# Gates of a selective scan: three of four channel groups go from VectorE to ScalarE and GpSimd

## The chip, the core and the metric

One core of a Trainium2 chip runs the whole program. The metric is the device time of one execution in microseconds (us), the median of several executions. Engines are named as in the profile: PE (TensorE; PEld are its weight loads), DVE (VectorE), ACT (ScalarE), POOL (GpSimd) and SP (which only issues transfers).

## The reference

The input x is 2 sequences of 2048 rows of 256 numbers. After a layer norm, two branches are computed, and their sum is added to x. One branch is a mixture of 16 experts, two chosen for each row. The other is a selective scan over 512 channels with 16 states each:

```
xz = x @ W_in;  x_in, z = split(xz)
u = silu(causal_conv4(x_in) + conv_b)
delta = softplus(dt_lr @ W_dt + b_dt)          # dt_lr, B, C = split(u @ W_xproj)
h_t = exp(delta_t * A) * h_{t-1} + delta_t * u_t * B_t
y_t = sum_n h_t[:, n] * C_t[n]  +  D_skip * u_t
out = (y * silu(z)) @ W_out
```

The change touches the last product, `y * silu(z)`, called the gate here.

## The kernel before

**Chunks and units.** The 4096 rows are cut into 8 chunks (0 to 7) of 512 rows. A chunk has 4 channel groups (`dc` = 0 to 3) of 128 channels, which lie on the partitions, and each group has 16 states. One state of one group of one chunk is a unit, a tile of 128 x 512: 64 units for each chunk, 512 in all. A unit goes through four engines:

- ACT computes the decay exp(delta * A) into `hb`, a ring of 12 units (L846). In program order it is 6 units ahead.
- DVE multiplies du by B into `psB` (L1632) and runs the scan in place in `hb` (L1643), unit after unit.
- POOL multiplies two units at a time by C into `hc`, a ring of 6 units (L658, called a pair here). Ten of the 256 pairs are DVE's (L1652).
- PE adds each unit of `hc` to the sum of its group with four transposing matmuls (L1150, `sum_unit`), four units later in its program. Groups take turns in two PSUM banks, `psY[dc % 2]`. Before its first unit a group's bank is started with D_skip * u (L1163, `dskip`).

ACT can write unit g of `hb` only when POOL has read unit g - 12, and POOL can write unit g of `hc` only when PE has summed unit g - 6.

**Slots.** Everything else is woven in by hand. Each engine's program is a loop over chunks and slots 0 to 63 (one for each unit), and the tables `AT`, `AT0` (chunk 0) and `AT7` (chunk 7) say after which slot an engine does which step; a name that `AT0` or `AT7` lacks is taken from `AT`. A slot is a place in the order of each engine's program, not a time: an engine gets there when all before it is done, and each engine executes strictly in order. The steps that matter here:

- **The projections of the next chunk.** They share one bank, `psA`, so PE and ACT alternate on it: x_in, convolution and silu (L1169, L1177 on PE, L780, L792, L799 on ACT), z (L1225 on PE, L869 and L874 on ACT, the last with silu at slot 28), and at slots 50 to 61 and 3 of the next chunk the four delta projections (`d_mm`, L1213 on PE), each followed by ACT's relu, exp and ln in the scratch tile `tmpA` (L828, L830, L835) and DVE's `d_max` (L1457), which reads `psA` and `tmpA`. `d_mm` of one group waits for `d_max` of the group before.
- **The gate** (L1659 on DVE): `zs[:, :, group] *= psY[dc % 2]`. It waits for silu(z) and for the last sum of its group. Groups 0 to 2 stand at slots 30, 45, 54 (`AT`), 34, 41, 52 (`AT0`) and 37, 41, 53 (`AT7`), and group 3 at slot 3 of the next chunk (slot 2 of chunk 7). It also frees its bank for the next but one group's `dskip`.
- **The output of a chunk.** `y_tr` on PE (L1233) transposes the gated tile once all its groups are gated, `y_copy` on ACT (L885), `o_mm` on PE (L1240), `o_copy` on ACT (L893) into `om`, four times, and then one accumulating transfer issued by POOL (L712) adds `om` to the output. For chunks 0 to 6 this is done in slots 4 to 17 of the next chunk. For chunk 7, three groups are done inside the chunk from slot 48 on, the last after the loop (L1429, L1438, L1695).
- **The experts.** 20 groups of 4 tiles, from unit 93 on: PE L1249, L1264, L1267, L1276, L1286, L1290, ACT L899, L906, L956, L967 (gelu, with a table load ahead and behind), L980. POOL adds each tile to the output with an indirect transfer (L707); each such transfer waits until the one before has landed, and an accumulating transfer of a chunk counts in the same row. In chunks 0 and 1 POOL also scatters 64 + 16 row tiles (L673, L681).

POOL also multiplies delta by u (L666, 128 x 512, both operands in SBUF), four times in each chunk.

## Time and profile before

| | |
|---|---|
| time, median of 3 executions | 1123.73 us (1122.23 to 1125.07) |
| profiled execution, first to last instruction (its span) | 1114.4 us |
| median less span: launch and end, outside of the trace | 9.3 us |
| busy share of the span | DVE 93%, PE 84%, POOL 79%, ACT 78% |
| mean granted clock of PE | 0.925 of full |

No time of its own is on record for the profiled execution beyond its span; the 9.3 us are taken as constant. All times in the trace are us from the first instruction. A row of a timeline is start, duration, engine, line, operation and count of a merged run of instructions; in brackets stands how long the engine sat idle before it, and what released it. The loop over chunks begins at about 62 us and ends at about 1105 us; chunk 5, which is read closely below, runs on DVE from about 723 to 848 us.

### The profile page before, as it was taken

To read this page: it belongs to the slowest core of one execution; us is meant where nothing else is said; L and a number is where in the kernel's file an instruction comes from. 1 tells how busy PE (TensorE), PEld (TensorE's weight loads), DVE (VectorE), ACT (ScalarE), POOL (GpSimd) and SP (SyncE) were. 2 spreads that over 40 slices of the span, in tenths; PEclk is the share of its full clock that TensorE was granted. 3 is DMA by queue.
4 is the path that set the end of the run, shared out by engine and by line. 5 is a ranking of instruction groups with operands and counts; after the bars stand their busy time and mean duration, and the time that the engine had idled before them with its cause. 6 is when DMAs were issued, how large, how long until landed. Compare 5 with 4: busy or idle time off the path is not lost.

```text
span 1114.4 us, 16950 instructions
## 1 busy us (share of the span) xinstructions
PE 930.9 (84%) x4575; PEld 630.4 (57%) x4575; DVE 1036.3 (93%) x1304; ACT 867.0 (78%) x1841; POOL 881.2 (79%) x570
## 2 busy tenths in 40 slices
PE   5947766587979999789998999899989999787776
PEld 3424434454656656566666766576656665565564
DVE  7999999799999988997899979999999999899995
ACT  4574788465897799767999699978998798976981
POOL 7178999599777887858787878887897886877995
PEclk9968986698999999899999999799998999899988
DMA  9496568953484544824457553763367443764313
GB/s 328 175 342 227 161 194 290 331 183 92 117 283 153 114 102 143 307 49 95 119 166 278 104 139 75 274 190 72 81 191 266 100 105 92 243 213 114 77 20 66
DMA packets 119367, 185.86 MB, mean 167 GB/s; under 512 B 12012, under 2 KB 104344, under 8 KB 111016
## 3 DMA queue, kind: packets, MB, share of 16 engines
q1 hardware_dynamic: 87120, 144.60, 38.8%
q0 software_dynamic: 19584, 25.26, 13.1%
q10 hardware_dynamic: 12568, 14.93, 4.4%
q8 instruction: 36, 0.59, 0.2%
q14 instruction: 59, 0.48, 0.1%
HBM read 146.34 MB, written 42.60 MB: 170 GB/s over the span
## 4 chain that ended last, share of the span: by engine, by line
PE 36%; issue 16%; ACT 15%; DVE 13%; POOL 11%; DMA 5%; ACTq 2%; SPq 1%; POOLq 0%; DVEq 0%
DVE hb L1643 10%; POOL hc L658 7%; PE psY L1150 7%; PE psA L1177 5%; PE psC L1290 4%; ACT hb L846 4%; PE psC L1240 3%; PE psA L1225 3%; PE psA L1169 2%; PE psE L1267 2%; ACT hnT L967 2%; DVE psB L1632 2%; POOL out L707 2%; DMA Cb<-bc_d 2%; DMA xs_d<-xg,slots 2%
## 5 line engine op out<-in xcount | busy, mean ns | idle before, releaser
L658 POOL TENSOR_TENSOR hc<-hb,Cb 128x1024 f32<-128x1024 f32 x246 | 623.8, 2630 | 83.3 <-PE psY L1150 64.4
L1643 DVE TENSOR_TENSOR_SCAN hb<-hb,carry,psB 128x512 f32<-128x512 f32 x384 | 471.8, 1263 | 7.7 <-ACT hb L846 6.1
L1150 PE MATMUL psY<-ident,hc 128*128 128x128 f32 x2048 | 306.9, 291 | 76.3 <-POOL hc L658 76.2
L846 ACT ACTIVATE hb<-delta,aneg 128x512 f32<-128x512 f32 x512 | 351.5, 716 | 21.7 <-POOL hc L658 15.7
L1150 PEld LDWEIGHTS psY<-ident,hc 128*128 128x128 f32 x2048 | 255.1, 150 | 191.0 <-POOL hc L658 109.4
L1632 DVE TENSOR_TENSOR psB<-Bb,psU 128x512 f32<-128x512 f32 x510 | 323.7, 679 | 0.5 <-DMA Bb<-bc_d 0.5
L707 POOL DMA_INDIRECT out<-yo,idx x80 | 128.0, 1600 | 55.3 <-DMA out<-yo,idx 18.0
L1643 DVE TENSOR_TENSOR_SCAN hb<-hb,psB 128x512 f32<-128x512 f32 x128 | 149.2, 1200 | 2.1 <-ACT hb L846 2.1
L1177 PE MATMUL psA<-ux,dgw 128*128 128x512 f32 x232 | 113.7, 610 | 3.0 <-ACT ux L786 2.0
L1290 PE MATMUL psC<-w2r,hnT 128*128 128x256 f32 x320 | 90.0, 430 | 0.0
L1267 PE MATMUL psE<-w1r,xgT 128*128 128x256 f32 x320 | 82.9, 404 | 0.0
L1290 PEld LDWEIGHTS psC<-w2r,hnT 128*128 128x128 f32 x320 | 63.9, 210 | 18.5 <-issue 10.0
L1267 PEld LDWEIGHTS psE<-w1r,xgT 128*128 128x128 f32 x320 | 59.3, 195 | 16.2 <-issue 9.3
L1169 PE MATMUL psA<-xnT,win 128*128 128x512 f32 x116 | 59.0, 626 | 11.2 <-ACT zs L876 5.0
L967 ACT ACTIVATE hnT<-hnT,vecs 128x128 f32<-128x128 f32 x160 | 64.2, 481 | 1.2 <-issue 0.7
L1225 PE MATMUL psA<-win,xnT 128*128 128x512 f32 x128 | 61.2, 600 | 3.0 <-ACT zs L869 2.2
L1240 PE MATMUL psC<-wout,ygT 128*128 128x256 f32 x248 | 59.8, 383 | 1.2 <-ACT ygT L885 0.8
L1177 PEld LDWEIGHTS psA<-ux,dgw 128*128 128x128 f32 x232 | 41.4, 198 | 31.9 <-issue 26.3
L673 POOL DMA_INDIRECT xs_d<-xg,slots x37 | 40.9, 1104 | 19.2 <-DMA xg<-xn_d 11.4
L1213 PE MATMUL psA<-xr,rows 16*128 16x512 f32 x60 | 40.7, 763 | 15.0 <-DVE delta L1457 14.3
L980 ACT ACTIVATE yo<-psC,wv 128x256 f32<-128x256 f32 x80 | 33.3, 468 | 21.2 <-PE psC L1290 21.2
L666 POOL TENSOR_TENSOR du<-delta,ux 128x512 f32<-128x512 f32 x31 | 44.6, 1438 | 6.6 <-DVE delta L1457 4.4
(235 smaller groups left out, 1205.8 us busy)
## 6 DMA issues: line engine op xcount, KB each, us to landing
Bb<-bc_d SPq DMA_DIRECT2D x32, 1024.0 KB, 6.7
Cb<-bc_d SPq DMA_DIRECT2D x32, 1024.0 KB, 7.5
w1r<-w1c_d SPq DMA_DIRECT2D x80, 256.0 KB, 2.8
w2r<-in_L_ffn_W SPq DMA_DIRECT2D x80, 256.0 KB, 3.5
xg<-xs_d SPq DMA_DIRECT2D x20, 516.0 KB, 5.8
xg<-xn_d SPq DMA_DIRECT2D x37, 128.0 KB, 2.9
Bb<-in_L_attn_x SPq DMA_DIRECT2D x8, 512.0 KB, 7.5
xn_d<-hb SPq DMA_DIRECT2D x8, 512.0 KB, 8.9
```

The costliest lines, as they stand in the source:

```text
L658: pool.tensor_tensor(hc[:, k:k + 2, :], hb[:, g % HR:g % HR + 2, :], Cb[:, n:n + 2, :], ALU.mult).then_inc(s_g, 1)
L707: pool.indirect_dma_start(out=out[:, :], out_offset=bass.IndirectOffsetOnAxis(ap=idx[:, g % 2, j:j + 1], axis=0), in_=yo[:, j, :], in_offs ...
L846: act.activation(hb[:, g % HR, :], delta[:, dc, :], ACT.Exp, scale=aneg[:, dc, n:n + 1]).then_inc(s_exp, 1)
L967: ins = act.activation(hnT[:, j, kc, :], hnT[:, j, kc, :], ACT.Gelu, scale=g1t[:, bass.ds(e, 1), kc], bias=be1t[:, bass.ds(e, 1), kc])
L1150: mm = pe.matmul(y[:, tt * P:(tt + 1) * P], hc[:, g % GR, tt * P:(tt + 1) * P], ident[:, :], start=False, stop=(n == NS - 1), is_transpose ...
L1177: mm = pe.matmul(bank[:, :], dgw[:, dc, k, :], x_of(p, dc)[:, k:k + T], start=(k == 0), stop=(k == KW - 1))
L1225: mm = pe.matmul(psA[:, :], xnT[:, c % 2, kc, tt * P:(tt + 1) * P], win[:, 1, kc, :], start=(kc == 0), stop=(kc == KC - 1))
L1240: mm = pe.matmul(psC[:, 0:D], ygT[:, dc, :], wout[:, dc, :], start=(dc == 0), stop=(dc == dc_out(c) - 1))
L1267: mm = pe.matmul(psE[:, a * D:(a + 1) * D], xgT[:, a, kc, :], w1r[:, a, kc, :], start=False, stop=(kc == KC - 1), skip_group_check=True)
L1290: mm = pe.matmul(psC[:, a * D:(a + 1) * D], hnT[:, 2 * h + a, kc, :], w2r[:, 2 * h + a, kc, :], start=False, stop=(kc == KC - 1), skip_gro ...
L1632: dve.tensor_tensor(psB[g % 2][:, :], Bb[:, n, :], psU[:, :], ALU.mult).then_inc(s_dbu, 1)
L1643: dve.tensor_tensor_scan(h, h, psB[g % 2][:, :], first, ALU.mult, ALU.add).then_inc(s_scan, 1)
```

## The change

DVE keeps the gate of group 3. For groups 0 to 2, ACT copies the sum out of its bank into SBUF (`y_evict`, slots 21, 37 and 53 of every chunk), and POOL multiplies `zs` by the copy, in place (`gate`, slots 30, 42 and 57; in chunks 0 and 7 the slots of before stay). No new buffer is made: the copy of groups 0 and 1 goes to `tmpA`, that of group 2 to the first half of `om`. So ACT's copy of group 1 waits for POOL's gate of group 0, and the relu of the next chunk's delta waits for POOL's gate. `dskip` now waits for ACT's copy instead of DVE's gate, and `y_tr` waits for POOL's gates.

```
-    "gate": [30, 45, 54, 3],
+    "gate": [30, 42, 57, 3],
...
+    "yev": [21, 37, 53],
...
+        def y_free(j):
+
+            c, dc = divmod(j, DC)
+            return (s_gate, c + 1) if dc == DC - 1 else (s_yev, c * (DC - 1) + dc + 1)
+
+        def yraw(dc):
+
+            return om[:, 0:2, :].rearrange("p a d -> p (a d)") if dc == 2 else tmpA[:, :]
...
+            def gate(c, dc):
+                pool.wait_ge(s_z, c + 1)
+                pool.wait_ge(s_zc, (c + 1) * TT)
+                pool.wait_ge(s_yev, c * (DC - 1) + dc + 1)
+                z = zs[:, :, dc * P:(dc + 1) * P]
+                pool.tensor_tensor(z, z, yraw(dc).rearrange("p (a b) -> p a b", a=TT), ALU.mult).then_inc(s_gp, 1)
...
+                        for dc in at(c, "gate", s, 0, DC - 1):
+                            gate(c, dc)
...
+                if p > 0 and dc < 2:
+                    act.wait_ge(s_gp, (p - 1) * (DC - 1) + dc + 1)
                 act.activation(tmp, bank_d(p, dc)[:, :], ACT.Relu, bias=col(bneg, dc), scale=-1.0).then_inc(s_de, 1)
...
+            def y_evict(c, dc):
+
+                act.wait_ge(s_tr, c * UN + (dc + 1) * NS)
+                if dc == 0:
+                    act.wait_ge(s_delta, (c + 1) * DC)
+                elif dc == 1:
+                    act.wait_ge(s_gp, c * (DC - 1) + 1)
+                elif c > 0:
+                    act.wait_ge(s_acc, 16 * ADD_TURN["chunk", c - 1, 0])
+                act.activation(yraw(dc), psY[dc % 2][:, :], ACT.Copy).then_inc(s_yev, 1)
...
             def dskip(c, dc):
                 j = c * DC + dc
                 if j >= 2:
-                    pe.wait_ge(s_gate, j - 1)
+                    pe.wait_ge(*y_free(j - 2))
...
             def y_tr(c, tt):
                 bank_c("y", c, tt)
-                pe.wait_ge(s_gate, c * DC + dc_out(c))
+                pe.wait_ge(s_gp, (c + 1) * (DC - 1))
+                if dc_out(c) == DC:
+                    pe.wait_ge(s_gate, c + 1)
...
-            def gate(c, dc):
+            def gate(c):
+                dc = DC - 1
                 dve.wait_ge(s_z, c + 1)
                 dve.wait_ge(s_zc, (c + 1) * TT)
-                dve.wait_ge(s_tr, c * UN + (dc + 1) * NS)
+                dve.wait_ge(s_tr, (c + 1) * UN)
```

**ACT in chunk 5, around slot 37.** The rows are ACT's order there, first before, then changed (lines of the changed file are larger; L800 and L1000 are the L780 and L967 of before).

```order
L780 ACTIVATE ux<-psA 128x512
L786 ACTIVATE ux<-psA 128x3
L963 TENSOR_LOAD etab
L963 ISA x2
L967 ISA
L967 REGISTER_ALU
L967 ACT_TABLE_LOAD
L967 ACTIVATE hnT<-hnT,vecs 128x128
```

```order
L800 ACTIVATE ux<-psA 128x512
L806 ACTIVATE ux<-psA 128x3
L885 ACTIVATE tmpA<-psY 128x512
L996 TENSOR_LOAD etab
L996 ISA x2
L1000 ISA
L1000 REGISTER_ALU
L1000 ACT_TABLE_LOAD
L1000 ACTIVATE hnT<-hnT,vecs 128x128
```

The copy of group 1 now stands between ACT's part of the convolution input and the gelu of an expert group with its table load.

**POOL in chunk 7, from slot 36 to the end.** Before, then changed; L658 and L669 are the pairs, L707 and L725 the experts' adds, L712 and L730 the add of the chunk, L684 the gate.

```order
L658 TENSOR_TENSOR hc<-hb,Cb 128x1024 x2
L707 DMA out<-yo,idx 4225x256
L658 TENSOR_TENSOR hc<-hb,Cb 128x1024 x3
L707 DMA out<-yo,idx 4225x256
L658 TENSOR_TENSOR hc<-hb,Cb 128x1024
L707 DMA out<-yo,idx 4225x256
L658 TENSOR_TENSOR hc<-hb,Cb 128x1024 x2
L707 DMA out<-yo,idx 4225x256
L658 TENSOR_TENSOR hc<-hb,Cb 128x1024 x2
L707 DMA out<-yo,idx 4225x256
L658 TENSOR_TENSOR hc<-hb,Cb 128x1024
L712 DMA out<-om 128x4x256
```

```order
L684 TENSOR_TENSOR zs<-zs,tmpA 128x4x128
L669 TENSOR_TENSOR hc<-hb,Cb 128x1024
L725 DMA out<-yo,idx 4225x256
L669 TENSOR_TENSOR hc<-hb,Cb 128x1024 x3
L725 DMA out<-yo,idx 4225x256
L669 TENSOR_TENSOR hc<-hb,Cb 128x1024
L725 DMA out<-yo,idx 4225x256
L669 TENSOR_TENSOR hc<-hb,Cb 128x1024
L684 TENSOR_TENSOR zs<-zs,om 128x4x128
L669 TENSOR_TENSOR hc<-hb,Cb 128x1024
L725 DMA out<-yo,idx 4225x256
L669 TENSOR_TENSOR hc<-hb,Cb 128x1024 x2
```

The pair between the last two experts' adds of the first piece (`x2`) is parted by the gate of group 2 in the second: it now stands between pair 52 and pair 54. The gates of groups 0 and 1 stand a little earlier.

**PE in chunk 7, at slot 51.** Before, then changed, with the semaphores that each waits for (`s_g`: POOL's pairs, `s_gate`: DVE's gates, `s_gp`: POOL's gates).

```order
L1150 MATMUL psY<-ident,hc 128x128 [waits s_g]
L1150 MATMUL psY<-ident,hc 128x128 x3
L1233 MATMUL psC<-ident,zs 128x128 [waits s_gate,s_c]
L1233 MATMUL psC<-ident,zs 128x128 x2
L1150 MATMUL psY<-ident,hc 128x128 [waits s_g]
L1150 MATMUL psY<-ident,hc 128x128 x3
```

```order
L1185 MATMUL psY<-ident,hc 128x128 [waits s_g]
L1185 MATMUL psY<-ident,hc 128x128 x3
L1270 MATMUL psC<-ident,zs 128x128 [waits s_gp,s_c]
L1270 MATMUL psC<-ident,zs 128x128 x2
L1185 MATMUL psY<-ident,hc 128x128 [waits s_g]
L1185 MATMUL psY<-ident,hc 128x128 x3
```

The order on PE is the same; the first `y_tr` of chunk 7, which stands between the sums of units 47 and 48, waits for POOL's third gate instead of DVE's.

## Rows read from the trace of the kernel before

**Rows 1.** The page: busy time of each engine, share of the span, instructions

```profile
PE 930.9 (84%) x4575; PEld 630.4 (57%) x4575; DVE 1036.3 (93%) x1304; ACT 867.0 (78%) x1841; POOL 881.2 (79%) x570
```

**Rows 2.** Groups by line: shapes xcount | busy us, mean ns | idle before <-releasers

```profile
L658 POOL TENSOR_TENSOR hc<-hb,Cb 128x1024 f32<-128x1024 f32 x246 | 623.8, 2630 | 83.3 <-PE psY L1150 64.4 <-DVE hb L1643 17.6
L1643 DVE TENSOR_TENSOR_SCAN hb<-hb,carry,psB 128x512 f32<-128x512 f32 x384 | 471.8, 1263 | 7.7 <-ACT hb L846 6.1 <-ACT carry L858 1.5
L1632 DVE TENSOR_TENSOR psB<-Bb,psU 128x512 f32<-128x512 f32 x510 | 323.7, 679 | 0.5 <-DMA Bb<-bc_d 0.5
...
L1659 DVE TENSOR_TENSOR zs<-zs,psY 128x512 f32<-128x512 f32 x32 | 21.4, 669 | 29.1 <-ACT zs L874 17.0 <-PE psY L1150 10.1 <-ACT zs L876 2.0
...
L869 ACT ACTIVATE zs<-psA 128x512 f32<-128x512 f32 x24 | 14.3, 595 | 10.0 <-PE psA L1225 10.0
```

**Rows 3.** POOL's line L666: duration ns min/median/max, first and last start

```profile
L666 POOL TENSOR_TENSOR du<-delta,ux x31: 1085/1284/1926, 92.0 to 1045.0; 128x512 f32<-128x512 f32 x31
```

**Rows 4.** Busy by window: PE, PEld, DVE, ACT, POOL, clock, DMA share, GB/s

```profile
269.00:299.00 30.00, 26.27 (x121) 15.77 (x120) 30.00 (x36) 21.46 (x42) 24.07 (x16) 0.94 0.42 125
781.00:813.00 32.00, 29.83 (x139) 19.21 (x138) 30.32 (x37) 31.18 (x61) 26.35 (x18) 1.00 0.34 80
813.00:844.00 31.00, 25.86 (x120) 16.41 (x119) 31.00 (x37) 28.23 (x57) 28.80 (x15) 0.79 0.78 248
```

**Rows 5.** Timeline, chunk 5 at slots 30 to 40: DVE, ACT, PE, POOL

```profile
784.51 0.69 DVE L1659 TENSOR_TENSOR zs<-zs,psY 128x512 f32<-128x512 f32 x1 [1.68 <-ACT zs L874]
...
796.44 1.28 ACT L967 ACT_TABLE_LOAD   x1
...
802.23 0.60 ACT L899 ACTIVATE xgT<-psC 128x512 f32<-128x512 f32 x1
...
802.89 0.39 PE L1286 MATMUL psC<-rows,pick 6*128 6x512 bf16 x1 [1.29 <-ACT xgT L899]
...
808.02 2.36 POOL L658 TENSOR_TENSOR hc<-hb,Cb 128x1024 f32<-128x1024 f32 x1 [5.02 <-PE psY L1150]
```

**Rows 6.** Timeline, chunk 5 at slots 54 to 60: POOL, then PE

```profile
832.25 7.52 POOL L658 TENSOR_TENSOR hc<-hb,Cb 128x1024 f32<-128x1024 f32 x3
841.47 2.36 POOL L658 TENSOR_TENSOR hc<-hb,Cb 128x1024 f32<-128x1024 f32 x1 [1.71 <-DVE hb L1643]
...
835.22 1.11 PE L1150 MATMUL psY<-ident,hc 128*128 128x128 f32 x4 [1.56 <-POOL hc L658]
837.89 2.07 PE L1213 MATMUL psA<-xr,rows 16*128 16x512 f32 x2 [1.56 <-DVE delta L1457]
```

**Rows 7.** Timeline, end of chunk 0: POOL, ACT, DVE

```profile
187.17 1.81 POOL L673 DMA_INDIRECT xs_d<-xg,slots  x1 [0.17 <-issue]
...
204.42 0.20 ACT L923 ACTIVATE xg<-meta 128x2 f32<-128x2 f32 x1 [10.93 <-DMA xs_d<-xg,slots]
...
207.26 0.75 DVE L1457 SCALAR_TENSOR_TENSOR delta<-psA,vecs,tmpA 128x512 f32<-128x512 f32 x1 [7.64 <-ACT tmpA L835]
```

**Rows 8.** Timeline of POOL, from the end of chunk 6 to the end

```profile
980.49 1.58 POOL L707 DMA_INDIRECT out<-yo,idx  x1 [3.26 <-DMA out<-yo,idx]
...
1028.90 1.68 POOL L707 DMA_INDIRECT out<-yo,idx  x1 [5.22 <-DMA out<-om]
...
1059.89 2.37 POOL L658 TENSOR_TENSOR hc<-hb,Cb 128x1024 f32<-128x1024 f32 x1 [0.83 <-PE psY L1150]
...
1085.97 2.35 POOL L658 TENSOR_TENSOR hc<-hb,Cb 128x1024 f32<-128x1024 f32 x1 [0.25 <-PE psY L1150]
...
1093.05 2.35 POOL L658 TENSOR_TENSOR hc<-hb,Cb 128x1024 f32<-128x1024 f32 x1 [0.60 <-DVE hb L1643]
...
1099.69 1.39 POOL L712 DMA_DIRECT2D out<-om  x1
```

**Rows 9.** Timeline of PE, chunk 7 at its first y_tr

```profile
1082.48 0.52 PE L1233 MATMUL psC<-ident,zs 128*128 128x128 f32 x3 [4.36 <-DVE zs L1659]
```

More of the change, by code:

```diff
@@ L386, in build @@
         s_c = sem("s_c")
+        s_yev, s_gp = sem("s_yev"), sem("s_gp")
         s_xT, s_xi, s_xq, s_xp, s_xe, s_u, s_xd, s_xr, s_bco = (sem(n) for n in (
@@ L1106, in _ @@
                         z_silu(c)
+                    for dc in at(c, "yev", s):
+                        y_evict(c, dc)
                     if c > 0:
@@ L1424, in _ @@
                 sum_unit(g)
-            pe.wait_ge(s_gate, NC * DC)
+            pe.wait_ge(s_gate, NC)
             pe.wait_ge(s_c, len(C_TURN))
@@ L1683, in _ @@
                                 d_max(c, 3)
-                        for dc in at(c, "gate", s, 0, DC - 1):
-                            gate(c, dc)
                         if c > 0:
                             for _ in at(c, "gate", s, DC - 1, DC):
-                                gate(c - 1, DC - 1)
-            gate(NC - 1, DC - 1)
+                                gate(c - 1)
+            gate(NC - 1)
             dve.wait_ge(s_fa, 16)
```

## The prediction

> **What bounds the kernel now.** I read the page first. DVE is busy for 93% of the span, the other three for 78 to 84% [rows 1]. That asks for DVE to be relieved, but busy shares average over stages, so the second view was the groups by line. DVE's own two operations of a unit take 1263 and 679 ns, a pair of units nearly 3.9 us by these means, and POOL's pair 2630 ns [rows 2]. POOL has its other work (du products, indirect transfers) beside this, so it is not far behind. The same view says what DVE waits for at its gates: 17.0 us for silu(z), 10.1 us for PE's last sums, and 2.0 us for the last quarter of silu(z) [rows 2].
>
> The third view, busy time by window, shows two regimes. In chunk 1 DVE is busy for all of its 30.00 us while POOL has 6 us free (the first of [rows 4]). From chunk 2 on the experts run as well. In chunk 5 at slots 32 to 48 ACT is busy for 31.18 of 32.00 us, and at slots 48 to 63 POOL is busy for 28.80 of 31.00 (the second and third of [rows 4]). There the engines pass the lead around, and the timeline shows how. PE's work on the projections ends in silu(z), for which DVE's gate of group 0 waits 1.68 us [rows 5]. ACT then does a gelu between two table loads and one copy more; PE waits for that copy until 802.89, and POOL waits 5.02 us for PE until 808.02 [rows 5]. From there POOL works through until it waits for DVE at 841.47 [rows 6]. PE waits for POOL at 835.22 and right afterwards for DVE's `d_max` until 837.89, by 1.56 us [rows 6]. With that `d_mm` the next round of projections starts. So DVE is the last of the chain in chunk 5 by only 1.56 us.
>
> **What is removed.** 24 DVE gates of 669 ns, 16.1 us in all, and with them the waits for silu(z), 17.0 + 2.0 = 19.0 us [rows 2]; the 10.1 us stay, as I put them with group 3, whose gate stays. If DVE were the bound all along, this would give 35.1 us.
>
> **What is added.** On ACT, 24 copies of a 128 x 512 bank to SBUF. The like of it, L869, takes 595 ns [rows 2], so 14.3 us. On POOL, 24 products of 128 x 512 from two SBUF tiles. L666 is the same operation and shape: 1085 at least, 1284 in the middle, 1926 at most [rows 3]. The long ones overlap what follows, so I take 1.2 us, 28.8 us in all, with 1.1 and 1.9 as ends. No transfer is added.
>
> The GPSIMD Engine Reference of the Trainium skill, in its section on elementwise work, speaks against such a move: VectorE is roughly 2x faster, and a two-input operation costs about 2.6 cycles for each element there. That would be an estimate of 1.1 us for 512 elements at 1.2 GHz before dispatch, 26.6 us for 24. The trace agrees: 1284 against 669 ns is 1.9 times.
>
> **What of it lies on the path, chunk by chunk.**
>
> *Chunk 0.* POOL is in arrears with its scatter when chunk 0 ends: the scatter issued at 187.17 has landed when ACT goes on at 204.42, and DVE waits 7.64 us at `d_max` for what ACT was held from [rows 7]. Three gates push that scatter back by up to 3 x 1.2 = 3.6 us. The transfers around it are what it waits for, so its landing need not move as much. Bounds 0 and +3.6; I take the third of it, **+1.2**. DVE's own 2.0 us less there are lost in its wait.
>
> *Chunk 1.* DVE has no wait, POOL has room [rows 4]. 3 x 0.67 = **-2.0**. Nothing is given back before chunk 2's projections start, since they start from DVE's `d_max`.
>
> *Chunks 2 to 5.* By chunk 5. The gate of group 0 on POOL is covered: it ends before POOL's wait of 5.02 us [rows 5]. ACT's copy of group 1 stands directly before the table load at 796.44; all behind it is ACT's own work up to the copy for which PE waits 1.29 us [rows 5]. So 0.6 us pass on to PE and, at 808.02, to POOL. The gate of group 1 comes after 808.02 where POOL no longer waits: 1.2 us. Together +1.8 for pair 54, which ended at 832.25 + 7.52 / 3 = 834.8 [rows 6]. DVE by now is 1.68 + 3 x 0.67 = 3.7 us early, but PE must first sum unit 54. Its start moves from 837.89 only by 1.8 - 1.56 = **+0.2**, and DVE's earliness turns into a wait of `d_max` or of a scan. The gate of group 2 comes after pair 56 and falls into POOL's wait of 1.71 us at 841.47, so it costs nothing; without that wait it would cost 1.2. Four chunks: **+0.8**. The longest of the five waits for silu(z) has more to give than the others (17.0 us by five are 3.4 each, that of chunk 5 is 1.68). DVE can use of it only what decays ACT has in stock, so I take **-1.0** for all four chunks together, with -8 as the far end.
>
> *Chunk 6.* ACT's 0.6 us as before. The gate of group 2 falls into a row of transfers that wait for one another: POOL waits 3.26 us at 980.49 for the last one to land [rows 8], so it passes on, 1.2. **+1.8**.
>
> *Chunk 7.* POOL is released at 1028.90 by the add of chunk 6, and from there to the end its only waits over 0.2 us are 0.83, 0.25 and 0.60 us [rows 8]. DVE hardly holds it up. The gates of groups 0 and 1: 2.4 - 0.83 = +1.6. The third gate is the costliest. PE's first `y_tr` waited 4.36 us for DVE's gate until 1082.48 [rows 9], when POOL was at pair 52. Now this gate comes after pair 52. Behind the waiting `y_tr` on PE stand the sums from unit 48 on, and pair 54 may be written only after unit 49 is summed. So between pairs 52 and 54 come 1.2 us for the gate, then on PE 0.5 for the three matmuls of `y_tr` [rows 9] and, at that rate, some 1.0 for the eight of two sums: 2.7 where there was 0.25 [rows 8]. That is +2.4, less the 0.60 of waiting for DVE that goes away: +3.4 in all for POOL. The four rounds of `y_tr`, copy, `o_mm`, copy start some 6 us later than at 1082.48 (pair 52 ended 0.25 us before 1085.97, at 1085.7 [rows 8]; + 1.6 + 1.2 = 1088.5). They took until POOL could issue the add of the chunk at 1099.69 [rows 8], with little to spare, so the add comes later than POOL alone would have it, and all that ends the kernel with it. Bounds +3.4 and +6; I take **+4.5**.
>
> Sum: 1.2 - 2.0 + 0.8 - 1.0 + 1.8 + 4.5 = +5.3. The span of 1114.4 becomes 1119.7; with the 9.3 us around it that is 1129.0 us. The median of before is 1123.73 = 1114.4 + 9.3, so it is the same sum.
>
> **The rivals.**
>
> *DVE is what counts (faster).* For it speaks the 93% and that DVE is the last in line at 837.89 [rows 1, 6]. If POOL hides its gates, because its waits for PE shrink by as much as it is late, chunks 2 to 6 each gain 2.0 for the gates and 1.7 for the wait, less ACT's 0.6: 3.1 x 5 = 15.5. With -2.0 of chunk 1, +1.2 of chunk 0 and, since POOL keeps up, +1.6 in chunk 7, this gives 1123.7 - 14.7 = 1109.0. It decides where POOL can end pair 54 earlier by more than the 1.2 of a gate. Against it: POOL was busy from 808.02 on [rows 6], and 28.80 of 31.00 us [rows 4]. The full 35.1 us would be 1088.6, which I exclude, since ACT is already full at slots 32 to 48.
>
> *No change.* The shares in the middle chunks cancel, the longest wait for silu(z) gives 3 instead of 1, and the end costs its lower bound: about 1124.
>
> *ACT is what counts (slower by more).* ACT waits in order at each copy for PE's sum. If its three copies and their waits all lie on the way of the projections, six chunks pay 3 x 0.6 instead of 0.6, +7.2 more, and the gates take 1.9 us instead of 1.2 at the five places where they are not covered, +3.5 more: 1140. Against it: at slots 21 and 53 ACT has waits for PE to hide a copy in.
>
> **How the numbers follow.** Forecast (+1 to +11, 1125 to 1135) 0.48, faster 0.28, no change 0.16, slower by more 0.08. About 0.3% (3.4 us) is what a measurement can tell from no change. A small part of the forecast's case (up to +3.4) is within it, 0.06, and the no-change case gives 0.13 to same and 0.03 to faster. Faster 0.31, same 0.19, slower 0.50. The range reaches down to the faster rival (1109) and up to nearly the slower one: 1110 to 1137. The likeliest case's own range is 1125 to 1135.
>
> **What the profile after would show.** DVE busy some 16 us less, no more waits at gates 0 to 2, but longer waits at `d_max` (for ACT's ln) and for decays. POOL's gates near 1.2 us, ACT's copies near 0.6. POOL further behind DVE at slots 44 to 56. In chunk 7, PE waiting for POOL's gate at the first `y_tr` some 6 us later than before, then pair 54 waiting for PE, and the chunk's add issued about 5 us later. Wrong would be: chunks 2 to 6 shorter by 3 us each, POOL waiting for DVE rather than DVE for the others, or a chunk 0 that ends at a quite different time because its scatters landed otherwise.

## The result and the profile after

| | median | executions |
|---|---|---|
| before | 1122.98 us | 4 (1121.57 to 1125.07) |
| after | 1132.58 us | 4 (1131.94 to 1135.39) |
| ratio after / before | 1.0107, 95% interval [1.0074, 1.0141] | |

The changed kernel is slower by 1.07%, about 12 us. The ratio is not that of the two medians in the table, which lie 9.6 us apart (0.85%); its interval holds both. Here and below a per cent is that of the ratio on record, and us are worked out from it at 1120 us. The forecast said slower (1129.0, +5.3 us), its range held the time, and the size was half of what came.

Two things about the spans first. The profiled execution of after took 1135.39 us with a span of 1133.4: only 2.0 us lie around the span, not 9.3. So the profiled execution of before, with its span of 1114.4, took about 1116.4, some 7 us less than its median. Spans of the two profiles therefore differ by 19.0 us where the kernels differ by about 12. PE's mean granted clock was 0.925 in that execution of before, where 98 others of that kernel on three chips had 0.907 to 0.922, and 0.916 in that of after. Ratios below come from many executions; profiles are used for what happens within a stretch.

Busy time of each engine, from the page of after, which answers to [rows 1]:

```profile
PE 938.5 (83%) x4574; PEld 636.4 (56%) x4575; DVE 1030.4 (91%) x1280; ACT 877.4 (77%) x1865; POOL 909.1 (80%) x594
```

POOL has 27.9 us more and ACT 10.4 more. DVE has lost 24 gates of 669 ns and yet only 5.9 us. What it waits for is in its groups by line, the answer to [rows 2] (scan, `d_max`, gate of group 3, after busy and mean the idle time ahead):

```profile
L1680 DVE TENSOR_TENSOR_SCAN hb<-hb,carry,psB 128x512 f32<-128x512 f32 x384 | 473.2, 1269 | 28.9 <-ACT hb L868 21.4 <-ACT carry L891 7.5
L1680 DVE TENSOR_TENSOR_SCAN hb<-hb,psB 128x512 f32<-128x512 f32 x128 | 149.7, 1206 | 6.8 <-ACT hb L868 6.8
L1494 DVE SCALAR_TENSOR_TENSOR delta<-psA,vecs,tmpA 128x512 f32<-128x512 f32 x30 | 22.1, 738 | 23.7 <-ACT tmpA L857 23.7
L1697 DVE TENSOR_TENSOR zs<-zs,psY 128x512 f32<-128x512 f32 x8 | 5.4, 681 | 19.5 <-PE psY L1185 19.5
```

The same groups of the kernel before that [rows 2] lack (the scans of chunk 0, `d_max`, DVE's own pairs):

```profile
L1643 DVE TENSOR_TENSOR_SCAN hb<-hb,psB 128x512 f32<-128x512 f32 x128 | 149.2, 1200 | 2.1 <-ACT hb L846 2.1
L1457 DVE SCALAR_TENSOR_TENSOR delta<-psA,vecs,tmpA 128x512 f32<-128x512 f32 x30 | 22.0, 733 | 16.9 <-ACT tmpA L835 16.9
L1652 DVE TENSOR_TENSOR hc<-hb,Cb 128x1024 f32<-128x1024 f32 x10 | 16.9, 1691 | 3.8 <-PE psY L1150 3.5
```

The waits for silu(z) are gone. Scans waited 7.7 + 2.1 us, mostly for ACT's decays, and now 28.9 + 6.8; `d_max` 16.9 and now 23.7. DVE is early and stands waiting a little further on.

The durations of the added work, from the lines of POOL's gate and ACT's copy for groups 0 and 1 (min/median/max in ns):

```profile
L684 POOL TENSOR_TENSOR zs<-zs,tmpA x16: 1254/1740/1865, 145.7 to 1079.7; 128x512 f32<-128x512 f32 x16
...
L885 ACT ACTIVATE tmpA<-psY x16: 573/600/615, 113.5 to 1072.5; 128x512 f32<-128x512 f32 x16
```

The copy is the 0.6 us of the forecast. POOL's record of a gate often reads 1.8 us, but the gate at 1079.65 below is followed by a pair at 1080.89: 1.24 us. Wherever a pair follows a gate at once it starts 1.22 to 1.24 us after it. Before a transfer POOL takes longer (824.27 to 826.25 below), and it will matter that whoever waits for the gate's result waits for the end of the record.

Busy time by window, answering to the second and third of [rows 4]; the windows are moved by 4 and 8 us, about as chunk 5 is:

```profile
785.00:817.00 32.00, 30.23 (x137) 19.36 (x136) 31.97 (x37) 30.94 (x55) 26.78 (x18) 0.95 0.37 92
821.00:852.00 31.00, 24.69 (x120) 14.76 (x119) 28.49 (x34) 28.00 (x58) 30.50 (x17) 0.87 0.69 213
```

In the second of these, POOL is busy for 30.50 us of 31.00 (28.80 before) and DVE for 28.49 (31.00 before). The timeline of chunk 5, POOL, PE, ACT and DVE, answers to [rows 5, 6]:

```profile
824.27 1.82 POOL L684 TENSOR_TENSOR zs<-zs,tmpA 128x512 f32<-128x512 f32 x1
826.25 1.59 POOL L725 DMA_INDIRECT out<-yo,idx  x1 [0.17 <-issue]
...
830.28 0.66 PE L1185 MATMUL psY<-ident,hc 128*128 128x128 f32 x4 [1.25 <-POOL hc L669]
...
833.22 0.38 ACT L939 ACTIVATE xgT<-psE 128x256 f32<-128x256 f32 x1 [1.45 <-PE psE L1304]
...
818.99 1.28 DVE L1680 TENSOR_TENSOR_SCAN hb<-hb,carry,psB 128x512 f32<-128x512 f32 x1 [2.02 <-ACT carry L891]
838.70 0.75 DVE L1494 SCALAR_TENSOR_TENSOR delta<-psA,vecs,tmpA 128x512 f32<-128x512 f32 x1 [2.51 <-ACT tmpA L857]
```

DVE had no wait at 818.99 before; its only one around there was the 1.68 us for silu(z) at slot 30 [rows 5]. Before, PE waited at slot 54 for DVE's `d_max` [rows 6]; now `d_max` waits for ACT (838.70), which had waited for PE (833.22), which had waited for POOL (830.28). The gate of group 1 at 824.27 lies in POOL's full stretch.

Timeline of chunk 7, POOL, PE and DVE, answering to [rows 8, 9]:

```profile
1079.65 1.83 POOL L684 TENSOR_TENSOR zs<-zs,tmpA 128x512 f32<-128x512 f32 x1
1080.89 2.90 POOL L669 TENSOR_TENSOR hc<-hb,Cb 128x1024 f32<-128x1024 f32 x1
...
1097.85 2.92 POOL L669 TENSOR_TENSOR hc<-hb,Cb 128x1024 f32<-128x1024 f32 x1
1100.15 1.84 POOL L684 TENSOR_TENSOR zs<-zs,om 128x512 f32<-128x512 f32 x1
1104.86 2.35 POOL L669 TENSOR_TENSOR hc<-hb,Cb 128x1024 f32<-128x1024 f32 x1 [2.87 <-PE psY L1185]
...
1102.13 0.87 PE L1270 MATMUL psC<-ident,zs 128*128 128x128 f32 x3 [8.25 <-POOL zs L684]
1102.79 4.24 PE L1185 MATMUL psY<-ident,hc 128*128 128x128 f32 x20
...
1123.92 0.69 DVE L1697 TENSOR_TENSOR zs<-zs,psY 128x512 f32<-128x512 f32 x1 [13.62 <-PE psY L1185]
```

This is what the forecast drew: PE's first `y_tr` waits for POOL's gate (8.25 us instead of 4.36), and the pair behind the gate then waits 2.87 us for PE. DVE, done early, waits 13.62 us for the last sum.

Two rows of before belong beside this, POOL's pair 52 and a window at PE's first matmuls after its wait (PE's granted clock is the last number but two):

```profile
1082.77 2.95 POOL L658 TENSOR_TENSOR hc<-hb,Cb 128x1024 f32<-128x1024 f32 x1
...
1082.40:1083.30 0.90, 0.82 (x8) 0.85 (x9) 0.90 (x2) 0.26 (x1) 0.90 (x2) 1.00 0.00 0
```

The same window after:

```profile
1102.10:1104.80 2.70, 2.67 (x13) 2.70 (x14) 2.70 (x4) 1.10 (x2) 0.00 (x0) 0.50 0.02 6
```

Before, `y_tr` ran at full clock (2.4 GHz); after, having waited 8.25 us, PE did `y_tr` and the sums that pair 54 needs at the lower of its two levels (1.2 GHz).

### The profile page after: what moved, and what is told of

The parts are those of the page before. It is cut to its first block and busy times, and to the rows that moved or that the text cites. A ratio compares the mean times of both kernels' runs of the same rounds, so it can differ in the third digit from the quotient of the medians.

```text
span 1133.4 us, 16997 instructions
## 1 busy us (share of the span) xinstructions
PE 938.5 (83%) x4574; PEld 636.4 (56%) x4575; DVE 1030.4 (91%) x1280; ACT 877.4 (77%) x1865; POOL 909.1 (80%) x594
## 5 line engine op out<-in xcount | busy, mean ns | idle before, releaser
L669 POOL TENSOR_TENSOR hc<-hb,Cb 128x1024 f32<-128x1024 f32 x246 | 629.6, 2648 | 85.0 <-PE psY L1185 62.4
L1680 DVE TENSOR_TENSOR_SCAN hb<-hb,carry,psB 128x512 f32<-128x512 f32 x384 | 473.2, 1269 | 28.9 <-ACT hb L868 21.4
L725 POOL DMA_INDIRECT out<-yo,idx x80 | 128.0, 1599 | 50.7 <-issue 16.8
L1000 ACT ACTIVATE hnT<-hnT,vecs 128x128 f32<-128x128 f32 x160 | 64.2, 481 | 1.0 <-issue 0.6
L926 ACT ACTIVATE om<-psC 128x256 f32<-128x256 f32 x32 | 12.2, 382 | 49.0 <-PE psC L1277 46.6
L1277 PEld LDWEIGHTS psC<-wout,ygT 128*128 128x128 f32 x248 | 45.9, 195 | 7.4 <-ACT ygT L918 2.1
```

Of the source, the lines that this page charges most:

```text
L669: pool.tensor_tensor(hc[:, k:k + 2, :], hb[:, g % HR:g % HR + 2, :], Cb[:, n:n + 2, :], ALU.mult).then_inc(s_g, 1)
L725: pool.indirect_dma_start(out=out[:, :], out_offset=bass.IndirectOffsetOnAxis(ap=idx[:, g % 2, j:j + 1], axis=0), in_=yo[:, j, :], in_offs ...
L1000: ins = act.activation(hnT[:, j, kc, :], hnT[:, j, kc, :], ACT.Gelu, scale=g1t[:, bass.ds(e, 1), kc], bias=be1t[:, bass.ds(e, 1), kc])
L1277: mm = pe.matmul(psC[:, 0:D], ygT[:, dc, :], wout[:, dc, :], start=(dc == 0), stop=(dc == dc_out(c) - 1))
L1680: dve.tensor_tensor_scan(h, h, psB[g % 2][:, :], first, ALU.mult, ALU.add).then_inc(s_scan, 1)
```

## The experiments

All kernels are made from one that has both kinds of gate and a list that says which are moved. A gate that is not moved stands on DVE at its slot of before, and who waits for it is switched with it. With an empty list every engine's order of instructions is that of before, with the full list that of after. Each ratio is to the kernel before on the same chip, with its 95% interval. There are twelve, on three chips: chunk 7 only, all but chunk 7, gates left out and products alone on the first; copies alone, group 2 of chunk 7, group 1 kept and group 0 alone on the second; the other four on the third.

```
+MOVED = [(c, dc) for c in range(NC) for dc in range(DC - 1) if moved(c, dc)]
...
+            return (s_yev, MOVED_N[c, dc]) if (c, dc) in MOVED_N else (s_gate, KEPT_N[c, dc])
```

### Which chunks: only chunk 7, and all but chunk 7

```
+moved = lambda c, dc: c == NC - 1
```

> Only chunk 7's three gates are moved to ACT and POOL; chunks 0 to 6 are as before. My theory (the end is the costliest place: POOL has no slack left there and PE's first y_tr now waits for a gate behind pair 52) says most of the loss is here. The prediction priced it at +4.5 us; the trace after the change, where POOL's shift against before grows by some 8 us between slot 32 of chunk 7 and the end, says +8, so 1127 to 1131. Rival (the loss builds up evenly, chunk by chunk, from the copies and the products): an eighth of the 9.6 us, about 1124.

Measured: 1.0056 [1.0027, 1.0085].

```
+moved = lambda c, dc: c < NC - 1
```

> The complement: chunks 0 to 6 moved, chunk 7's gates stay on VectorE. My theory: 1132.6 less 5 to 8 = 1125 to 1128, what stays being the losses of chunks 0, 3 and 6. Rival (even): 1131. A third view (VectorE relief works and only the end spoils it): at or below 1120.

Measured: 1.0058 [1.0037, 1.0078]. The two add up to 1.14%, the whole change has 1.07%. So about half of the loss is in chunk 7 (6.3 us, with 3.0 to 9.5 in its interval) and half in the seven chunks ahead of it (6.5 us, 4.1 to 8.7). For these seven my own sum had 0.8 us.

### What the relief alone is worth: gates of groups 0 to 2 left out

This kernel leaves `y * silu(z)` out for groups 0 to 2; nothing takes its place, PE's `y_tr` waits for silu(z) instead, and `dskip` of a bank that such a group leaves waits for no gate.

```
             def gate(c, dc):
-                if (c, dc) not in KEPT_N:
+                if dc < DC - 1:
                     return
```

> The relief of VectorE by itself: the 24 gates of groups 0 to 2 are left out altogether (the product with silu(z) is missing there), with nothing added on ACT or POOL; PE's y_tr waits for silu(z) directly. My theory (VectorE is last in line by only 1 to 2 us in each chunk, except in chunk 1 and at the end): -6 to -14 us, 1109 to 1117. Rival (VectorE is the bound all along): the full 35 us, 1088 to 1093. If this came out near 1123, even free gates would bring nothing.

Measured: 0.9984 [0.9962, 1.0007]. This is the run that surprised me most. 16.1 us of work and 19.0 us of waits are taken from the engine that is busy for 93% of the span, and 1.8 us come back, which can't be told from none (the interval reaches from 4.3 us won to 0.8 lost). Its groups by line, of DVE, say where they went:

```profile
L1694 DVE TENSOR_TENSOR_SCAN hb<-hb,carry,psB 128x512 f32<-128x512 f32 x384 | 471.8, 1263 | 27.3 <-ACT hb L878 20.5 <-ACT carry L901 6.6
L1694 DVE TENSOR_TENSOR_SCAN hb<-hb,psB 128x512 f32<-128x512 f32 x128 | 149.4, 1202 | 5.8 <-ACT hb L878 5.8
L1508 DVE SCALAR_TENSOR_TENSOR delta<-psA,vecs,tmpA 128x512 f32<-128x512 f32 x30 | 22.0, 734 | 24.8 <-ACT tmpA L867 22.4 <-issue 2.4
...
L1712 DVE TENSOR_TENSOR zs<-zs,psY 128x512 f32<-128x512 f32 x8 | 5.4, 676 | 14.6 <-PE psY L1196 14.6
```

Scans wait 33.1 us where it was 9.8, `d_max` 24.8 where it was 16.9, the gate of group 3 14.6 where PE's sums had 10.1: 35.7 us of new waits for 35.1 freed (in a span that is 5.6 us longer, so some of it is of this execution). These are the waits of after, although nothing was added to ACT and POOL. In chunk 2 the exchange can be read row by row. DVE before:

```profile
394.27 0.69 DVE L1659 TENSOR_TENSOR zs<-zs,psY 128x512 f32<-128x512 f32 x1 [2.40 <-ACT zs L874]
...
403.94 2.45 DVE L1643 TENSOR_TENSOR_SCAN hb<-hb,carry,psB 128x512 f32<-128x512 f32 x2 [0.71 <-ACT hb L846]
```

and without the gate:

```profile
404.43 2.45 DVE L1694 TENSOR_TENSOR_SCAN hb<-hb,carry,psB 128x512 f32<-128x512 f32 x2 [3.82 <-ACT hb L878]
```

2.40 of waiting, 0.69 of gate and 0.71 of waiting become one wait of 3.82 us at a scan 10 us later, and that scan starts at 404.43 instead of 403.94.

### What the added work alone costs: products alone, copies alone

DVE keeps all its gates. In the first kernel POOL does 24 products of 128 x 512 at the gates' slots, from a constant into `tmpA` or `om`, which are overwritten later; those who write there wait for it. In the second ACT makes the 24 copies; nothing reads them, but DVE's gate of the group waits for the copy, so this is a little more than ACT's time.

```
+                            w = dgw[:, 0, :, :].rearrange("p a b -> p (a b)")
+                            pool.tensor_tensor(yraw(dc), w, w, ALU.mult).then_inc(s_gp, 1)
```

> POOL's load by itself: before, with 24 further products of 128x512 on POOL at the slots of the change, which read constant weights and write the free scratch; nobody needs their results (only the next writer of the scratch waits for them). VectorE's gates stay, ACT makes no copies. My theory: POOL has no room in chunk 0, after slot 40 of the middle chunks and in chunk 7; VectorE still takes 3.7 us more per chunk, so the middle ones hide most: +3 to +6, 1126 to 1129. Rival 1 (POOL's idle time takes them all): 1123. Rival 2 (POOL is the bound, every product counts): +29, 1152.

Measured: 1.0031 [1.0012, 1.0049]: 3.5 us for 24 x 1.24 = 29.8 us of POOL's time. POOL hides nearly nine tenths.

```
-                        if (c, dc) in MOVED_N:
-                            y_evict(c, dc)
+                        y_evict(c, dc)
...
             def gate(c, dc):
+                if dc < DC - 1:
+                    dve.wait_ge(s_yev, c * (DC - 1) + dc + 1)
```

> ACT's load by itself: before, with ACT's 24 copies of the banks at the slots of the change; nothing reads the copies. VectorE keeps its gates (they wait for the copy only because two engines may not read a bank at once), POOL has no products. Theory 'in order on ACT' (a copy stands before a gelu with its table loads, and waits for PE's sum, so it delays the projections and the experts): 0.6 us for each of chunks 2 to 6, +3 to +5, that is 1.003 to 1.0045 of before. Rival (ACT, busy for 78%, hides them): within 0.1% of before.

Measured: 1.0039 [1.0018, 1.0060]: 4.4 us for 14 us of ACT's time. Relief (-0.16), products (+0.31) and copies (+0.39) add up to +0.54%, against 1.07% for the change. Three errors add up in the sum, so the gap of 0.5% is only just clear of noise. It fits that the other half exists when the parts are coupled: a gate behind its copy, and PE behind the gate. In chunk 7 this shows (below).

### Chunk 7: gate of group 2 alone, then the same two slots earlier

```
+moved = lambda c, dc: (c, dc) == (NC - 1, 2)
```

> Only the gate of group 2 of chunk 7 is moved. Theory 'PE's first y_tr stands behind pair 52 now': it is most of what chunk 7 costs (6.3 us with all three moved), +3 to +5, 1.003 to 1.0045. Rival (chunk 7 pays for POOL's load, each gate alike): a third of 6.3, +2.

Measured: 1.0038 [1.0021, 1.0055], by the middle values two thirds of what all three gates of chunk 7 cost.

```
 AT7
-    "pgate": [37, 41, 53],
+    "pgate": [37, 41, 51],
+    "yev": [21, 37, 51],
```

> Only the gate of group 2 of chunk 7 is moved, as in the run that put it behind pair 52 (ratio 1.0038), but POOL's product now stands between pair 50 and pair 52 and ACT's copy two units earlier. Theory A (what costs is the place: PE's first y_tr cannot start until pair 52 and the gate are done, and pair 54 then waits for the sums behind it): y_tr starts some 3.9 us earlier than in that run (pair 50 ended 1088.7 there, y_tr began 1094.1), pair 54 does not wait 2.83 us, and the ratio falls to 1.0005 to 1.0018. Theory B (what costs is that ACT and POOL do a copy and a product more at the end at all): no difference, 1.003 to 1.0045.

Measured: 1.0012 [0.9988, 1.0035]. The value is the one of theory A; the interval reaches into theory B's, so the timeline must help. First POOL and PE with the gate behind pair 52:

```profile
1089.91 2.92 POOL L678 TENSOR_TENSOR hc<-hb,Cb 128x1024 f32<-128x1024 f32 x1
1092.21 1.83 POOL L693 TENSOR_TENSOR zs<-zs,om 128x512 f32<-128x512 f32 x1
1096.87 2.35 POOL L678 TENSOR_TENSOR hc<-hb,Cb 128x1024 f32<-128x1024 f32 x1 [2.83 <-PE psY L1196]
...
1094.14 0.88 PE L1282 MATMUL psC<-ident,zs 128*128 128x128 f32 x3 [8.11 <-issue]
```

and with the gate ahead of it:

```profile
1086.59 2.94 POOL L679 TENSOR_TENSOR hc<-hb,Cb 128x1024 f32<-128x1024 f32 x1
1088.91 1.83 POOL L694 TENSOR_TENSOR zs<-zs,om 128x512 f32<-128x512 f32 x1
...
1091.93 5.26 POOL L679 TENSOR_TENSOR hc<-hb,Cb 128x1024 f32<-128x1024 f32 x2
...
1090.85 0.85 PE L1283 MATMUL psC<-ident,zs 128*128 128x128 f32 x3 [5.21 <-issue]
```

`y_tr` starts 3.3 us earlier, and pairs 52 and 54 follow one another in one merged row, without the 2.83 us of waiting.

A second reading is worked out from the profiles: how much longer than in the kernel before it takes from the scan after slot 62 of chunk 6 to the end of the span.

| kernel | us longer |
|---|---|
| after; only chunk 7's three gates | 8.5; 8.9 |
| group 2 of chunk 7; the same two slots earlier | 5.9; 1.1 |
| products alone; copies alone | -0.9; 0.5 |
| gates left out | 4.6 |
| six kernels whose chunk 7 is that of before | 0.0, 1.3, 1.7, 1.9, 3.7, 4.4 |

The last two rows say how far single profiles can be trusted. The three gates stand clear of them, the gate behind pair 52 somewhat above, and the early one is inside. With the rows of PE and POOL above, the place is what cost: the same product and the same copy, two slots earlier, hold nobody up. And neither products nor copies cost anything here that shows, as long as PE does not wait for them.

### Chunks 0 to 6: which group

```
+moved = lambda c, dc: c < NC - 1 and dc != 1
```

> Groups 0 and 2 of chunks 0 to 6 moved, group 1 and all of chunk 7 stay on VectorE. With group 1 moved as well it was 1.0058 of before. Theory (group 1 is the dear one: its copy stands before the gelu, its product comes when POOL no longer waits): it falls by 5 x 1.8 less what others absorb, to 1.000 to 1.002. Rival (chunks 0 and 1 or the third group are the dear ones): stays at 1.004 to 1.006.

Measured: 0.9980 [0.9960, 1.0000]. Against 1.0058 with group 1 moved as well: the gate of group 1 in company with the others costs 0.78%, 8.7 us, by the middle values more than the whole loss of these chunks.

```
+moved = lambda c, dc: dc == 1 and c < NC - 1
```

> Only group 1's gates of chunks 0 to 6 are moved, groups 0, 2 and 3 and chunk 7 stay on DVE. Leaving group 1 out of the move of chunks 0 to 6 took the ratio from 1.0058 to 0.998. Theory A (group 1 costs by its own, its copy on ACT stands before the gelu and its product falls in a busy stretch of POOL): 1.005 to 1.008. Theory B (it costs only in company: copy of group 1 waits for POOL's gate of group 0, and three products add up where two fit): 0.998 to 1.002.

Measured: 1.0035 [1.0013, 1.0058], between the two theories: by itself group 1 costs about half of that, and the rest in company with groups 0 and 2.

```
 AT
-    "yev": [21, 37, 53],
+    "yev": [21, 40, 53],
...
-    "pgate": [30, 42, 57],
+    "pgate": [30, 44, 57],
```

> All three gates of chunks 0 to 6 moved, chunk 7 kept, as in the run with 1.0058, but ACT's copy of group 1 stands at slot 40 (behind the gelu of chunks 4 to 6 and its table loads) instead of 37, and POOL's product at slot 44 instead of 42. Theory A (the copy ahead of the gelu pushes PE, and PE pushes POOL, and that is most of group 1's cost): 0.999 to 1.003. Theory B (the place of the copy is not it, the cost is POOL's third product or the bank that comes free late): 1.004 to 1.007.

Measured: 1.0019 [1.0002, 1.0036], just disjoint from 1.0058 [1.0037, 1.0078], which another chip gave. That is theory A's range, so the place of the copy and the gate matters.

Where group 1 acts can be seen in chunk 5. ACT with group 1 on DVE (chunks 0 to 6, groups 0 and 2 moved), and DVE's waits there:

```profile
796.90 0.59 ACT L810 ACTIVATE ux<-psA 128x512 f32<-128x512 f32 x1
...
797.56 1.28 ACT L1010 ACT_TABLE_LOAD   x1
...
811.20 0.20 ACT L901 ACTIVATE carry<-hb 128x4 f32<-128x4 f32 x1
...
811.44 1.28 DVE L1692 TENSOR_TENSOR_SCAN hb<-hb,carry,psB 128x512 f32<-128x512 f32 x1 [1.34 <-ACT carry L901]
829.02 0.75 DVE L1506 SCALAR_TENSOR_TENSOR delta<-psA,vecs,tmpA 128x512 f32<-128x512 f32 x1 [0.38 <-ACT tmpA L867]
846.32 0.75 DVE L1506 SCALAR_TENSOR_TENSOR delta<-psA,vecs,tmpA 128x512 f32<-128x512 f32 x1 [1.12 <-ACT tmpA L867]
```

and with group 1 moved too:

```profile
801.88 0.59 ACT L810 ACTIVATE ux<-psA 128x512 f32<-128x512 f32 x1
...
802.40 0.61 ACT L895 ACTIVATE tmpA<-psY 128x512 f32<-128x512 f32 x1
803.03 1.28 ACT L1010 ACT_TABLE_LOAD   x1
...
816.67 0.20 ACT L901 ACTIVATE carry<-hb 128x4 f32<-128x4 f32 x1
...
816.91 1.28 DVE L1692 TENSOR_TENSOR_SCAN hb<-hb,carry,psB 128x512 f32<-128x512 f32 x1 [2.02 <-ACT carry L901]
835.00 0.75 DVE L1506 SCALAR_TENSOR_TENSOR delta<-psA,vecs,tmpA 128x512 f32<-128x512 f32 x1 [0.89 <-ACT tmpA L867]
853.50 0.75 DVE L1506 SCALAR_TENSOR_TENSOR delta<-psA,vecs,tmpA 128x512 f32<-128x512 f32 x1 [2.33 <-ACT tmpA L867]
```

From L810 to the table load it is 0.66 us in the first and 1.15 in the second; the 0.49 us of the copy are still there 14 us later at the `carry` for which DVE waits (811.20 - 796.90 = 14.30, 816.67 - 801.88 = 14.79). DVE's three waits add up to 2.84 us in the first and 5.24 in the second, 2.40 more for 0.67 of work taken away: group 1 costs a net 1.7 us in this chunk.

The next table is worked out: the end of DVE's scan of a unit less that of the same unit before, in us.

| scan after slot | chunk 4: 26, 32, 50, 62 | chunk 5: 26, 32, 50, 62 | chunk 6: 26, 32, 50, 62 |
|---|---|---|---|
| groups 0, 1, 2 moved (chunks 0 to 6) | 5.2, 1.1, 4.9, 5.9 | 6.1, 3.7, 5.2, 5.6 | 6.5, 3.6, 6.7, 8.4 |
| groups 0 and 2 | 1.3, -2.9, 0.4, 1.0 | 0.7, -1.7, -0.2, -0.3 | -0.6, -3.6, -0.9, -0.5 |
| group 1 alone | 3.4, 3.1, 3.0, 5.7 | 6.3, 6.3, 5.7, 7.5 | 8.3, 8.0, 8.5, 9.9 |
| chunk 7's group 2 alone | 4.8, 4.9, 4.9, 4.9 | 5.0, 5.0, 5.0, 5.0 | 5.1, 5.1, 5.1, 5.1 |

The last row is the control: through chunk 6 its engines do what they did before, and it stands 5 us off, from chunks 2 and 3 (it stands at -0.6 at the end of chunk 1 and at 1.5 at the end of chunk 2), but stays level from here on. The two other kernels that differ from before in chunk 7 alone start chunk 4 at 3.9 and 7.5 and move by -0.3 and +0.3 until the end of chunk 6, with steps of up to 0.7 between; in chunk 1 all three stay level. So chunk 1 and chunks 4 to 6 can be read from single profiles, to within some 0.7 us, and chunks 2 and 3 hardly. The rows with group 0 moved gain 2.4 to 4.2 us at slot 32 (no gate there and no wait for silu(z)) and have lost most of it at slot 50. With group 1 moved too, more is lost than was won. The growth of the first row less that of the second, from slot 26 of chunk 4 to the end of chunk 6, is (8.4 - 5.2) - (-0.5 - 1.3) = 5.0 us of group 1's 8.7.

The profile does not show the gain of the late copy: in its profiled execution (1128.72 us, the slowest of its 12) the three waits of chunk 5 are 1.53, 0.49 and 2.82, 4.84 us together against 5.24. How much of the 0.39% is the copy's place and how much the product's stays open.

### Groups 0 and 2 of chunks 1 to 6, and group 0 alone

```
+moved = lambda c, dc: dc == 0 and 1 <= c < NC - 1
```

> Only group 0 of chunks 1 to 6 moved: the one for which VectorE waited for silu(z) (17 us in all), whose product on POOL falls into a wait for PE. Since leaving all gates out brought only 0.16%, my theory says that VectorE's waits just move: 0.999 to 1.001. Rival (this wait is worth something by itself and the other gates spoil it): 0.990 to 0.996, and then it is the version that beats both kernels.

Measured: 0.9991 [0.9969, 1.0014], no change that could be told.

```
+moved = lambda c, dc: dc != 1 and 1 <= c < NC - 1
```

> Groups 0 and 2 of chunks 1 to 6 moved, all else on DVE as before. The run with groups 0 and 2 of chunks 0 to 6 moved had 0.998 [0.996, 1.000]; with chunk 0 left alone too, nothing is delayed at the scatters. If that half of the move is worth something, 0.996 to 0.999; if DVE's relief is worth nothing in any stretch, as leaving three gates out altogether says (0.9984), 0.998 to 1.001.

Measured: 0.9963 [0.9943, 0.9983], median 1118.64 us against 1122.07. This version beats both kernels, with 12 gates of 24 moved. Why they gain, when leaving out all 24 gains no more, was not tried. PE's mean granted clock was 0.920 over its executions and 0.915 over those of before beside it, and within either kernel the executions with the higher clock are the shorter ones; how much of the gain goes with the clock is open.

## Why the prediction was right in sign and half in size

**Slower, in the range: right.** So were the durations: 0.60 for the copy, 1.24 between starts for POOL's gate where a pair follows. The GPSIMD Engine Reference of the Trainium skill, in its section on elementwise work, speaks against such a move; the result of the whole agrees (1.0107), that of half of the gates doesn't, since they were moved at a gain (0.9963).

**Chunk 7, +4.5: the mechanism right, the term rather too small.** It measured 0.56%, 6.3 us, with an interval that holds 4.5. Of this the gate of group 2 is 0.38%, 4.3 us (2.4 to 6.2), where I had 4.5 - 1.6 = 2.9 for it and the late add. By the times alone the term was not wrong; the rows show where it was short. From the start of pair 52 to that of pair 54 it was 3.20 us (1082.77 to 1085.97); I had 2.4 more, and it is 7.01 in after and 6.96 with group 2 alone, 3.8 more. Two prices were too low. PE can go on only when the gate's record has ended, 1.93 to 1.98 us after its start in three profiles (1100.15 to 1102.13 in after), and not after 1.2. And `y_tr` with two sums took 2.73 us until pair 54 (1102.13 to 1104.86), and not 1.5: I had priced it at the clock of before's `y_tr`, which was the full one, and after the long wait it was half of that. Against this the gate starts 2.30 us after pair 52 does, where I had waited for the end of its record. The early slot takes two thirds of the cost back by the middle values. Groups 0 and 1 are left with 0.18%, 2.0 us, by difference (forecast 1.6); that was not run.

**Chunk 5, +0.2 and a little for silu(z): right, as far as single profiles tell.** "DVE is the last of the chain in chunk 5 by only 1.56 us": with groups 0 and 2 moved, chunk 5 (slot 26 to slot 26 of the next) gains 0.7 + 0.6 = 1.3 us, and group 1 then costs 1.7 where I had 1.8. With all three the scans go from 6.1 to 6.5: +0.4.

**"Four chunks: +0.8": this is the step that failed.** I had read chunk 5 alone and carried its 1.56 us over to chunks 2 to 4, and to chunk 6 nothing. Chunks 0 to 6 together cost 0.58%, 6.5 us, where my terms give 1.2 - 2.0 + 0.8 - 1.0 + 1.8 = 0.8. In the profile of that run the scans lose 0.9 in chunk 4 (5.2 to 6.1), 0.4 in chunk 5 and 1.9 by the end of chunk 6 (6.5 to 8.4; forecast 1.8). That is 3.2 us against 0.2 + 0.2 + 1.8 - 0.5 = 1.7 forecast. The rest, some 3 us (with some 2 either way) where I had -0.9, would by difference lie in chunks 0 to 3. Chunks 0 and 1 have part of it (below), but the profiles can't confirm the sum: at slot 26 of chunk 4 this run stands at 5.2, and the three kernels that do the same as before up to there at 3.9, 4.8 and 7.5. For chunks 2 and 3 it stays open. What is shown is whose it is: the gate of group 1 in chunks 0 to 6 costs 0.78%, 8.7 us, in company with the others and 0.35% by itself, while groups 0 and 2 gain 0.2% (an interval that touches none) or, with chunk 0 left alone, 0.37%.

**Chunk 1, -2.0, "nothing is given back before chunk 2's projections start": wrong in part.** With the gates left out DVE gains 1.8 us from slot 26 to slot 56, its three gates, and gives 1.1 back by slot 62, at chunk 1's own `d_max`, which waits for ACT:

```profile
323.69 0.75 DVE L1508 SCALAR_TENSOR_TENSOR delta<-psA,vecs,tmpA 128x512 f32<-128x512 f32 x1 [0.95 <-ACT tmpA L867]
```

With the gates of chunks 0 to 6 moved 1.4 of 1.8 us are given back there, and in after 3.0, where the same `d_max` waits 2.85 us: -0.4 and +1.2 in place of -2.0. The delta projections of the next chunk are in this chunk's last slots, and DVE's earliness ends there.

**-1.0 for silu(z):** in chunk 2 all of the 2.40 us are returned at a scan 10 us later. For all of DVE's relief, everywhere, the run without gates has 1.8 us; I had 3.0 for chunk 1 and silu(z) alone, which its interval (up to 4.3) doesn't exclude.

**Chunk 0, +1.2,** was not measured by itself, but the profiles side by side say it was too little there. Against before, the scan after slot 62 of chunk 0 ends 1.6, 2.6 and 3.3 us later in the three runs with all of its gates moved, and 0.8 to 1.9 us earlier in the five others whose chunk 0 is before's: the two sorts don't overlap, and their means lie 3.6 us apart, which was my upper bound. By the end of chunk 2 the same three stand at 0.1 to 3.9 and the three that are still before's at 1.5 to 3.8 (before itself at 0), so how much of it lasts is open. In after, `d_max` waits 1.58 us at 203.81 where it was 7.64 at 207.26 [rows 7].

**The 9.3 us around the span** were wrong (2.0), but stood on both sides of the sum and changed nothing.

**The rivals.** That DVE counts (1109 us, 0.28) was far off, and I gave it too much: ACT at 31.18 of 32.00 us and POOL at 28.80 of 31.00 in [rows 4] already left DVE little to win. That ACT counts (1140, 0.08) has something to it: copies alone cost 4.4 us, no less than POOL's products (3.5), which take twice the time.

## What to carry to other kernels

An engine that is busy for 93% need not be worth relieving. Leave the work out altogether and time that, before you design where to put it: here that gave 0.16% [-0.07, 0.38], so there was little to win whatever the other engines did. It is a guide and no strict ceiling, since the version with 12 gates moved measured 0.37%, at the edge of that interval. When moving a set of equal operations, price each by its place and move only those that pay: 12 of 24 made the kernel faster by 0.37%, all 24 slower by 1.07%. A step on which an in-order engine stands waiting (here PE at `y_tr`) belongs ahead of its new engine's next long operation, not behind it. And price what stands behind a longer wait of PE at the lower clock too.

## What the runs showed of the hardware

On POOL a gate, a two-input product of 128 x 512 from SBUF, has a record of 1254 to 1865 ns. A pair that follows at once starts 1.22 to 1.24 us after it, whatever the record says, and a transfer 1.43 to 1.98 us after it; PE, waiting for the result, started 0.10 to 0.14 us after the end of the record in three profiles. So what such a product costs POOL and how long it holds up its reader are two numbers.

PE's granted clock after a wait differed. After 8.25 and 8.11 us of waiting it was at its lower level for all of the next matmuls that pair 54 needed (0.50), with `y_tr` and two sums in some 2.7 us. After 4.36 us, in before, the first eight matmuls ran at full clock and later ones at the lower level: 0.66 in the mean of 1082 to 1087 us.

DVE's own products of 128 x 1024 have the same median before and after, but not the same maximum (the line before, then after; min/median/max in ns):

```profile
L1652 DVE TENSOR_TENSOR hc<-hb,Cb x10: 1224/1326/3632, 67.9 to 439.1; 128x1024 f32<-128x1024 f32 x10
```

```profile
L1689 DVE TENSOR_TENSOR hc<-hb,Cb x10: 1224/1328/4825, 67.7 to 441.7; 128x1024 f32<-128x1024 f32 x10
```

They are busy for 16.9 us before and 22.6 us after (ten of 2265 ns in the mean), which is part of why DVE's busy time fell by 5.9 us and not by 16. Why a few of them take two to four times as long was not tried.

Executions of one kernel on one chip spread more than I had assumed: 35 of the kernel before lie between 1117.06 and 1128.70 us, and in three that do the same as before through chunk 6 the scans were 3.9, 4.8 and 7.5 us later by chunk 4.
